# Weighted values of a 16-head cross-attention in 32-column tiles of TensorE, four heads at a time, and a new order of the work

## The reference, cut to what matters

```python
x = x + jnp.tanh(g_xattn[0]) * _L0_xattn_ref(_layernorm(x), ctx, Wq, Wk, Wv, Wo, bo)
# inside:  q, k, v = x @ Wq.T, context @ Wk.T, context @ Wv.T       (16 heads of 64)
sim  = jnp.einsum('bihd,bjhd->bhij', q, k) * DH ** -0.5
attn = jax.nn.softmax(sim, axis=-1)
out  = jnp.einsum('bhij,bjhd->bihd', attn, v).reshape(b, nq, 1024) @ Wo.T + bo
```

## Time and profile before

| | |
|---|---|
| median of 3 runs | 3960.9 us (3960.36 to 3961.63) |
| the profiled execution: time, span | 3958.11 us, 3956.4 us |
| granted TensorE clock, mean over the span | 0.989 of full speed |
| PE busy, PE weight loads | 3859.5 us (98%), 3183.1 us (80%) |
| DVE, ACT, POOL busy | 2891.5 us (73%), 2158.1 us (55%), 1385.0 us (35%) |

### The profile page before, as it was taken

One profiled execution on the slowest core, in us unless ns is written; L12 is line 12 of the kernel. 1 busy time (PEld: TensorE's weight loads), 2 busy tenths in 40 slices (PEclk: granted clock), 3 DMA queues, 4 the chain that ended last, 5 costly groups with the idle time before them and its releaser, 6 DMA issues.

```text
span 3956.4 us, 91849 instructions
## 1 busy us (share of the span) xinstructions
PE 3859.5 (98%) x30740; PEld 3183.1 (80%) x30740; DVE 2891.5 (73%) x6494; ACT 2158.1 (55%) x4137; POOL 1385.0 (35%) x1557
## 2 busy tenths in 40 slices
PE   6999999999999999999999999999999999999958
PEld 5888888888888888888888888888888888888845
DVE  4777777777777777777777777777777777777746
ACT  4555555555555555555555555555555555555521
POOL 3333333333433433333333333343343343333310
PEclk8999999999999999999999999999999999999979
DMA  2000000000000000000000000000000000000001
GB/s 87 13 17 12 11 16 13 10 16 16 8 15 16 9 14 16 9 14 16 9 14 16 13 10 16 13 10 16 16 9 14 16 9 14 16 9 14 12 24 58
DMA packets 57906, 64.79 MB, mean 16 GB/s; under 512 B 5232, under 2 KB 54672, under 8 KB 57104
## 3 DMA queue, kind: packets, MB, share of 16 engines
q10 hardware_dynamic: 34688, 32.52, 2.7%
q1 hardware_dynamic: 23184, 31.81, 2.4%
HBM read 47.01 MB, written 17.30 MB: 16 GB/s over the span
## 4 chain that ended last, share of the span: by engine, by line
issue 63%; POOL 25%; PE 8%; DVE 2%; POOLq 1%; ACT 1%; DMA 0%; DVEq 0%; SPq 0%; ACTq 0%
POOL q_lo L484 7%; POOL q_lo L479 5%; POOL kmx L472 3%; PE g L696 2%; POOL y_x L455 2%; POOL x_res L441 2%; PE g L690 2%; POOL kbd_hi L463 1%; POOL kbd_lo L463 1%; POOL y_rstd L431 1%; POOL x_rstd L431 1%; PE scores L841 1%; POOLq L117 1%; PE scores L690 1%; POOL y_rstd L429 1%
## 5 line engine op out<-in xcount | busy, mean ns | idle before, releaser
L620 ACT ACTIVATE prob<-scores 120x1024 f32<-120x1024 f32 x512 | 510.7, 1023 | 238.6 <-PE scores L796 100.0
L1178 DVE SCALAR_TENSOR_TENSOR x<-g,lg_w,x 128x256 f32<-128x256 f32 x1024 | 495.0, 483 | 121.1 <-PE g L690 94.8
L639 ACT ACTIVATE inv<-scores 64x512 f32<-64x512 f32 x512 | 303.4, 593 | 465.2 <-PE scores L841 461.3
L841 PE MATMUL scores<-prob,vx 120*128 120x256 f32 x2048 | 532.8, 388 | 2.7 <-DVE an L1077 2.6
L1077 DVE TENSOR_TENSOR an<-scores,inv 64x256 f32<-64x256 f32 x1024 | 424.5, 415 | 147.2 <-ACT inv L641 140.3
L484 POOL TENSOR_TENSOR q_lo<-an,q_hi 128x256 fp32r<-128x256 f32 x512 | 368.3, 736 | 252.4 <-ACT q_hi L651 243.2
L535 ACT CAST q_hi<-g 128x512 fp32r<-128x512 f32 x256 | 150.5, 588 | 544.5 <-PE g L690 544.5
L690 PE MATMUL g<-ew_hi,yT_hi 128*128 128x512 f32 x1024 | 445.0, 435 | 0.0
L841 PEld LDWEIGHTS scores<-prob,vx 120*128 120x128 f32 x2048 | 374.6, 190 | 74.5 <-issue 3.7
L690 PE MATMUL g<-ew_hi,yT_lo 128*128 128x512 f32 x1024 | 404.3, 395 | 0.0
L690 PE MATMUL g<-ew_lo,yT_hi 128*128 128x512 f32 x1024 | 402.6, 393 | 0.0
(11 more groups left out here) (207 smaller groups left out, 9852.8 us busy)
## 6 DMA issues: line engine op xcount, KB each, us to landing
x_in<-in_x ACTq DMA_DIRECT2D x64, 256.0 KB, 2.9
out<-y_x SPq DMA_DIRECT2D x64, 256.0 KB, 2.1
ctx_in<-in_ctx ACTq DMA_DIRECT2D x128, 120.0 KB, 2.3
wk_s<-in_gu SPq DMA_DIRECT2D x8, 512.0 KB, 3.5
wk_s<-in_wk SPq DMA_DIRECT2D x1, 1024.0 KB, 5.2
prob<-in_wq SPq DMA_DIRECT2D x1, 1024.0 KB, 7.9
wv_s<-in_wv SPq DMA_DIRECT2D x1, 1024.0 KB, 10.5
vx<-in_wo SPq DMA_DIRECT2D x1, 1024.0 KB, 11.8
```

Source lines behind the costliest of these rows:

```text
L620: a.activation(prob[:, e % 2].rearrange("p o u s -> p (o u s)"), scores[0:NK, banks, :].rearrange("p o c -> p (o c)"), ACT.Exp, scale=scal ...
L639: a.activation(dst, sums, ACT.Ln).then_inc(logged.sem, 1)
L841: ins = t_.matmul(pv[p % 2][:, o * S:(o + 1) * S], vx[0:NK, 2 * p + o, :], prob[:, p // 2 % 2, o, p % 2, :], start=True, stop=True)
L1178: ins = v.scalar_tensor_tensor(out=x1[:, t, :], in0=ring.bank(Y_FFN[j])[:, o * D:(o + 1) * D], scalar=lg_w[:, t, 2 * n + o:2 * n + o + 1], ...
```

## The change

Values and sums are separate products. `vx` holds only the values (128 by 1024), and `ones` is a tile of 32 columns of ones. `x_pv` is now a step for a quad of four heads. It makes four matmuls of 32 columns for the sums, into rows 32j to 32j+31 of a `pv` bank for head j of the quad, and eight for the values, 32 features each, into one bank of the ring (row group j is head j, column half `a` is the half of its 64 features). One inverse (128 by 256) and one multiplication (128 by 512, the inverse used for both halves) serve four heads; the copy and the rest, too, are taken for four heads at once. The blocks of `an` and `q` now hold 32 features of each of four heads, so `wo` is loaded in that order, in eight DMAs in place of one. `x_pv` joins `FILLS`, so the values take four banks of the ring in a pass. Signals are counted by quads, those for keys and queries are separate, the second weight split moves from behind `n_k` 1 to behind `n_k` 0, and `ORDER` is new.

```diff
-    ("x_st", 0), ("n_load", 0), ("z_hi", 1), ("y_k", 0), ("y_ffn", 0), ("x_st", 1), ("x_pv", 0), ("z_out", 0),
-    ("x_mul", 0), ("y_ffn", 1), ("x_pv", 1), ("x_mul", 1), ("x_st", 2), ("x_pv", 2), ("n_stat", 0), ("y_ffn", 2),
...
+    ("x_st", 0), ("y_k", 0), ("y_ffn", 0), ("n_load", 0), ("z_hi", 1), ("n_stat", 0), ("y_ffn", 1), ("n_norm", 0),
+    ("y_ffn", 2), ("y_ffn", 3), ("y_ffn", 4), ("z_out", 0), ("y_ffn", 5), ("n_tr", 0), ("y_ffn", 6), ("y_ffn", 7),
+    ("x_st", 1), ("x_pv", 0), ("x_pv", 1), ("y_stat3", 0), ("x_mul", 0), ("x_hi", 0), ("x_st", 2), ("y_v", 0),
+    ("y_norm3", 0), ("x_mul", 1), ("y_tr3", 0), ("y_res", 0), ("x_st", 3), ("x_pv", 2), ("x_hi", 1), ("x_mul", 2),
+    ("x_pv", 3), ("x_mul", 3), ("n_ctx", 0), ("x_hi", 2), ("y_q", 0), ("x_hi", 3), ("n_k", 0), ("x_out", 0),
+    ("y_max", 0), ("x_out", 1), ("x_out", 2), ("y_max", 1), ("x_out", 3), ("p_stat", 0), ("n_q", 0), ("n_q", 1),
+    ("n_q", 2), ("p_norm", 0), ("y_maxt", 0), ("n_k", 1), ("y_maxt", 1), ("p_tr2", 0), ("n_q", 3), ("n_max", 0),
...
-        vx = sb("vx", [P, H, P])
+        vx, ones = sb("vx", [P, INNER]), sb("ones", [P, 32])
...
+                if n == 1:
+                    for row, a, block in wo_blocks:
+                        blocks = staged(n).rearrange("p (k n) -> p k n", n=D)[row:row + 32, a::2, :]
+                        sp.dma_start(blocks, block).then_inc(stage_in[n % 2], 16)
...
-            def x_pv(i, p):
-                x_mixed.wait(act, i, p + 1)
-                if p >= 2:
-                    x_attn.wait(act, i, p - 1)
-                invert(pv[p % 2][64:128, :], inv[:, p % 2, :], x_logged, x_recip, i, p + 1)
+            def x_pv(i, g):
+                x_mixed.wait(act, i, g + 1)
+                if g >= 2:
+                    ring.empty(act, i, X_PV[g - 2])
+                invert(pv[g % 2][:, 0:S], inv[:, g % 2, :], x_logged, x_recip, i, g + 1)
...
-                for o in range(2):
-                    ins = t_.matmul(pv[p % 2][:, o * S:(o + 1) * S], vx[0:NK, 2 * p + o, :], prob[:, p // 2 % 2, o, p % 2, :],
+                for j in range(4):
+                    ins = t_.matmul(pv[g % 2][32 * j:32 * j + 32, 0:S], ones[0:NK, :], prob[:, g % 2, j % 2, j // 2, :],
                                     start=True, stop=True)
                 ins.then_inc(x_mixed.sem, 1)
+                ring.to_fill(pe, i, X_PV[g])
+                for a in range(2):
+                    for j in range(4):
+                        col = (4 * g + j) * DH0 + 32 * a
+                        ins = t_.matmul(ring.bank(X_PV[g])[32 * j:32 * j + 32, a * S:(a + 1) * S], vx[0:NK, col:col + 32],
+                                        prob[:, g % 2, j % 2, j // 2, :], start=True, stop=True)
+                ring.has_filled(ins, X_PV[g])
...
+            def x_mul(i, g):
+                ring.full(dve, i, X_PV[g])
+                x_recip.wait(dve, i, g + 1)
+                if g >= 2:
+                    x_attn_lo.wait(dve, i, g - 1)
+                ring.has_emptied(v.tensor_tensor(an[:, 2 * (g % 2):2 * (g % 2) + 2, :],
+                                                 ring.bank(X_PV[g])[:].rearrange("p (a s) -> p a s", a=2),
+                                                 inv[:, g % 2, :].unsqueeze(1).broadcast_to([P, 2, S]), ALU.mult), X_PV[g])
```

More of the change, by code:

```diff
@@ L50 @@
 ORDER = (
-    ("x_st", 0), ("n_load", 0), ("z_hi", 1), ("y_k", 0), ("y_ffn", 0), ("x_st", 1), ("x_pv", 0), ("z_out", 0),
-    ("x_mul", 0), ("y_ffn", 1), ("x_pv", 1), ("x_mul", 1), ("x_st", 2), ("x_pv", 2), ("n_stat", 0), ("y_ffn", 2),
[L53 to L62, removed]
+    ("x_st", 0), ("y_k", 0), ("y_ffn", 0), ("n_load", 0), ("z_hi", 1), ("n_stat", 0), ("y_ffn", 1), ("n_norm", 0),
[5 more added lines that the diff above has]
+    ("n_q", 2), ("p_norm", 0), ("y_maxt", 0), ("n_k", 1), ("y_maxt", 1), ("p_tr2", 0), ("n_q", 3), ("n_max", 0),
+    ("p_gate", 0), ("y_st", 0), ("n_max", 1), ("p_lg", 0), ("n_v", 0), ("n_max", 2), ("y_mul", 0), ("p_load", 0),
+    ("n_maxt", 0), ("y_st", 1), ("y_pv", 0), ("n_max", 3), ("p_wt", 0), ("n_v", 1), ("y_pv", 1), ("n_maxt", 1),
+    ("p_eb", 0), ("y_mul", 1), ("p_ctx", 0), ("y_hi", 0), ("n_res", 0),
 )
@@ L65 @@
 FILLS = ("n_ctx", "n_tr", "n_k", "n_v", "n_q", "n_max", "n_maxt", "p_tr2", "p_gate", "p_lg", "p_ctx", "p_wt", "p_eb",
-         "y_pv", "y_k", "y_v", "y_ffn", "y_tr3", "y_q", "y_max", "y_maxt")
+         "x_pv", "y_pv", "y_k", "y_v", "y_ffn", "y_tr3", "y_q", "y_max", "y_maxt")
 NG = 4
@@ L93 @@
     "n_ctx", "n_tr", "p_tr2", "p_gate", "p_lg", "p_ctx", "p_wt", "p_eb", "y_k", "y_v", "y_tr3", "y_q"))
+X_PV = [("x_pv", g) for g in range(QUADS)]
 Y_PV = [("y_pv", m) for m in range(KD)]
@@ L229, in flamingo_stack @@
         prob = prob_rows[0:NK]
-        an, inv = sb("an", [P, 3, S]), sb("inv", [64, 2, 2 * S])
+        an, inv = sb("an", [P, 4, S]), sb("inv", [P, 2, S])
         x1 = sb("x1", [P, T, D])
@@ L344, in flamingo_stack @@
         stage = (prob_rows[:].rearrange("p a b c s -> p (a b c s)"), vx1[:])
+        wo_blocks = [(32 * j, a, wo[64 * (j % 2) + 32 * a:64 * (j % 2) + 32 * a + 32, j // 2::2, :])
+                     for j in range(4) for a in range(2)]
         def staged(n):
@@ L349, in flamingo_stack @@
         in_order = [step for step in ORDER if step[0][0] == "n"]
-        AFTER = (max(("n_ctx", 0), ("n_tr", 0), key=in_order.index), ("n_k", 1), ("n_q", 1), ("n_q", 3), in_order[-1])
+        AFTER = (max(("n_ctx", 0), ("n_tr", 0), key=in_order.index), ("n_k", 0), ("n_q", 1), ("n_q", 3), in_order[-1])
         def first(i):
@@ L470, in x_k @@
                     pool.wait_ge(dve_zeroed, 1)
-                x_hi.wait(pool, i, 2 + c)
+                x_khi.wait(pool, i, 1 + c)
                 g.tensor_tensor(kmx[:, 4 * c:4 * c + 4, :, :],
@@ L557, in x_k @@
             def x_k(i, c):
-                hi_of(x_hi, i, X_K[c], 4 * NK, flat(kT[0][:, 4 * c:4 * c + 4, :]))
+                hi_of(x_khi, i, X_K[c], 4 * NK, flat(kT[0][:, 4 * c:4 * c + 4, :]))
             def x_v(i, c):
-                if first(i):
-                    act.wait_ge(const_done, CONST)
                 ring.full(act, i, X_V[c])
-                ring.has_emptied(a.copy(vx[0:NK, 8 * c:8 * c + 8, 0:DH0],
-                                      ring.bank(X_V[c])[0:NK, :].rearrange("p (h d) -> p h d", d=DH0)), X_V[c])
+                ring.has_emptied(a.copy(vx[0:NK, 512 * c:512 * (c + 1)], ring.bank(X_V[c])[0:NK, :]), X_V[c])
             def x_q(i, c):
-                hi_of(x_hi, i, X_Q[c], 2 * S, flat(q[0][:, 2 * c:2 * c + 2, :]))
+                hi_of(x_qhi, i, X_Q[c], 2 * S, flat(q[0][:, 2 * c:2 * c + 2, :]))
                 x_qlo.wait(act, i, c - 1)
@@ L625, in x_st @@
                 if g >= 2:
-                    x_mixed.wait(act, i, 2 * g - 2)
+                    ring.full(act, i, X_PV[g - 2])
                 exp(g, slice(0, 2), SCALE0, x_probs)
```

60 lines of the change are left out of this document (26 added, 34 removed).

## The result

The changed kernel takes 3825.3 us (median of 4 runs, 3821.3 to 3827.7) where the kernel before took 3961.1 us beside it (3960.4 to 3961.6): a ratio of 0.9657 [0.9642, 0.9672], 136 us less.

The account below looks back on a forecast made before the run. TensorE's own instruction list was taken to bound each pass. A gain of 1.4 us a pass times 64 is 90 us, less 1 us at the start: 89 us, median 3872 us, range 3830 to 3915 us.

Parts of the forecast that it names:

- x_pv before, with what it makes late: Old products of x_pv: 32 times 0.22 us plus 0.2 us for two blocks behind scores, 7.2 us a pass.
- x_pv after: 24 groups: New products of x_pv: 96 instructions run four side by side, 24 groups at 0.22 us, 5.3 us a pass.
- x_pv after: edges: Entering and leaving the blocks of quads, and a slow successor: 0.6 us a pass.
- fewer and other neighbours: Four steps fewer to wait at and expert products in three blocks, not five: 0.1 us a pass gained.
- two blocks with 0.12 + 0.1 + 0.1 us, 0.6 us in all: Quads in twos behind scores: 0.12 us for leaving, 0.1 for entering, 0.1 for a slow successor, per block.
- rival C: New list also removes losses at blocks left alone: gain 1.8 to 2.4 us a pass, 3845 to 3807 us; chance 0.17.
- (6): Wait at p_tr2: three n_q and n_k 1 ahead, before four n_q and n_max 0, about as long.
- rival B: TensorE can't be handed small instructions fast enough: pass 1.2 us longer at 43 ns each, 4038 us; chance 0.06.
- Waits (1) to (5): Possible waits in the new list, at x_pv 1 and 3, x_st 3, y_tr3, x_out 1 and ring fills; new stalls 0.
- the bad case of (3): At y_tr3, the two xn take 2.68 us in place of 0.86 with POOL at work; 0.9 us are lost.
- The start: Output weights loaded in eight DMAs in place of one: +1 us once, between -2 and +6.
- The element-wise work: Inverses, copies, products and rests: ACT sheds 7 us, DVE 4 us, POOL under 1 us a pass; costed at nothing.

## Why the prediction was right, and where it was wrong

By its steps, in us a pass:

| step | predicted | measured |
|---|---|---|
| x_pv before, with what it makes late | 7.2 | 6.49 + 0.76 = 7.25 |
| x_pv after: 24 groups | 5.3 | 5.18 |
| x_pv after: edges | 0.6 | 0.27 |
| fewer and other neighbours | 0.1 | 0.39 |
| the gain | 1.4 | 2.19 |

**The step that failed is "two blocks with 0.12 + 0.1 + 0.1 us, 0.6 us in all".** Only 0.12 for leaving was real. The 0.1 for entering was read from the distance of 0.23 us behind the last scores of layer 1. It is the edge of the scores, 0.21 us behind their last group whatever follows, and it was there before x_pv before the change as well: 1927.98 to 1928.19 in the earlier trace rows. It was charged to the new kernel and not to the old one. The 0.1 for a slow successor was read behind a pair at 1928.97, but a quad's successor in the new list is x_st 2 or n_ctx. The first distance in x_st is 0.21 us behind anything, so nothing is late twice; the transposes of n_ctx take 0.18 us, and took 0.13 to 0.21 us in the kernel before. The Trainium skill, TensorEngine Tiling (Array Packing), section Key Properties, says that a change of the tiling mode drains TensorE. The trace agrees, but the distance between scores and values is paid once, and the prediction took it as a price of the new quads alone. This is 0.33 of the 0.79 us that were missed.

**The second part, 0.29 us, are the neighbours, taken at 0.1 us and measured at 0.39.** The transposes of xn alone shed 0.26 us, since none of their blocks is now in front of values or of scores of layer 1. Other kinds gave and took up to 0.45 us each, for 0.13 us net: n_v 0 shed 0.45 us, and the two y_maxt took as much, of which 0.37 us is the wait for xn that now stands behind the second. Such a figure is no price of a neighbour by itself, as the distance can pass on to the next kind: n_max 2, now behind n_v 0, takes 0.51 us to its second instruction, where the other n_max take 0.11 or 0.21. Why each kind changed stays open. The sum is what rival C had in mind, at a third to three quarters of its size (0.4 to 1.0 us wanted, beside the forecast's 1.4; 0.29 found). The time fell in C's range with other help: 1.80 of the 2.19 us came from x_pv and from the blocks that it made late, where 1.3 us were forecast.

**The third, 0.12 us, is 0.216 us for a group in place of 0.22**, rounded up from 1.76 / 8, with the sum of 24.

**The last, 0.05 us, is the price of before.** In the kernel before four blocks stood behind a pair (three of expert products and z_out), and each lost 0.19 us in its first distance, 0.76 us in all. The pairs in front of them were shorter in return, by about as much, so the 0.22 us each of the prediction held. The pair in front of x_st 2 took 0.96 us in place of 0.88, for which nothing was allowed.

The wait in front of p_tr2, which (6) called "about as long", is so: 0.03 us longer than before, by idle time and by distances.

One sum of rival B is off, without effect: its streams of 10.5 us (three x_st at 1.14, the groups with edges at 5.9, y_v 0.9 and y_tr3 0.5) add up to 10.7.

**What held.** TensorE bounds the pass: 56.29 of 56.51 us busy. Waits (1) to (5) brought no idle time in the pass, and the two xn of y_norm3 took 0.73 us, so the bad case of (3) didn't come. ACT has 26.9 us and DVE 40.4 us a pass, for 26 and 40 predicted. A quad of 24 instructions takes 1926.19 - 1924.87 = 1.32 us, under the 1.5 us at which B would have begun. The start is 2.0 us later at the first x_st (52.0 for 50.1 us), for 1 us predicted, and this is regained by the start of the third pass. The element-wise work was costed at nothing, and none of its engines bounds the pass. It may still be part of what allows the list: with the old products and the old element-wise work together, the same order costs 12.8 us a pass.

**Two theories and what is left of them.** The theory that the products bring the gain (with the old list: 0.72 us a pass) and the one that the list brings it (with the old products: a loss) are both wrong alone. That quads in one block save edges is shown by the run with n_ctx between quads, 0.33 us for one cut, and by 0.33 us around a lone quad. That every block in smaller tiles costs this isn't so. y_pv 1 stands alone in the changed kernel too:

```profile
1961.51 1.98 PE L699 MATMUL g<-wv_s,ctxT 128*120 128x512 f32 x4
1963.42 1.07 PE L862 MATMUL g<-prob,vx 120*32 120x256 f32 x16
1964.42 0.33 PE L780 MATMUL g<-ident,x_nm 128*128 128x128 f32 x1
1964.50 0.48 PE L922 MATMUL g<-eb,wT 128*128 128x256 f32 x2
```

It takes 1.00 us for four groups of 0.216, so 0.14 us of edge, and the last distance in front of it is 0.52 us in place of the 0.43 us that such an instruction takes between its own kind. But the transpose behind it isn't late (0.08 us, where one like it takes 0.11 us in front of the keys): some 0.2 us in all, not 0.33. What about the neighbours decides it stays open; no run varied them one by one. The 3.0 us of the end weren't followed up.

No run beat the changed kernel. The four that tried to remove its last wait (n_q 3, n_max 0 and twice y_max 1) all put a longer one in its place.

## What to carry to other kernels

When a block's edges are priced, look for the same edge in the kernel before: what the neighbour pays whatever stands beside it belongs to neither side of the sum. An order of work can be worth more than the products that it was made for (1.47 us a pass against 0.72 here), and may not be open to the old ones; only the two runs with one of the two changes each show this. In a list at 99% of TensorE each block is also the cover of someone's wait; before it is moved, name what waits behind it, and count the ring banks that it fills.

## What was unexpected of the hardware

- Products of 32 columns for four column groups run at nearly the same rate in turn (0, 1, 2, 3, 0, ...) and in twos (0, 0, 1, 1, ...): 5.46 and 5.56 us a pass for all of x_pv. The Trainium skill, TensorEngine Tiling (Array Packing), section Key Properties, says that tiles operate independently. This trace agrees, but for the 0.1 us.
- A wait of TensorE costs more than the idle time shown: 0.77 us for 0.51 us. The idle time is counted from the end of the instruction in front, at 0.39 us, but without a wait the next one starts after 0.23 us, 0.16 us before that end; and the first distance behind the wait is 0.34 us in place of 0.23. In front of p_tr2 it is 0.37 us for 0.21 us shown.
- Two DVE instructions of 128 by 256 take 0.73 us together, and 2.64 us while GpSimd works on float32 tiles; TensorE's only wait in a steady pass hangs on them. With y_max 1 behind n_q 0 they fall outside GpSimd's work and take 0.73 us.
